# A two-layer attention and expert kernel: the first sequence's tokens sorted into blocks of one expert each, with their rows, weights and first units ahead of the second sequence's chain

## The reference

```
topk_w, topk_idx = top_k(router(x), 2)              # weights made to sum to 1
gate = sum(one_hot(topk_idx, 8) * topk_w, axis=1)
h    = act(einsum('th,ehf->etf', x, W1) + b1)       # relu in layer one, gelu in layer two
y    = einsum('etf,efh->eth', h, W2) + b2
out  = einsum('te,eth->th', gate, y)
```

## Time and profile before

| what | value |
|---|---|
| median of three runs | 1223.13 us (1223.12 to 1223.13) |
| profiled execution, its own time | 1223.02 us |
| its span in the trace | 1221.2 us |
| mean granted PE clock | 0.986 |
| PE busy | 1105.6 us, 91% |
| DVE busy | 864.5 us, 71% |
| ACT busy | 777.3 us, 64% |
| POOL busy | 281.8 us, 23% |
| bytes moved | 57.71 MB, mean 47 GB/s |

### The profile page before, as it was taken

One profiled execution on the slowest core, in us unless ns is written; L12 is line 12 of the kernel. 1 busy time (PEld: TensorE's weight loads), 2 busy tenths in 40 slices (PEclk: granted clock), 3 DMA queues, 4 the chain that ended last, 5 costly groups with the idle time before them and its releaser, 6 DMA issues. The chain is left out here.

```text
span 1221.2 us, 24980 instructions
## 1 busy us (share of the span) xinstructions
PE 1105.6 (91%) x8797; PEld 605.1 (50%) x8872; DVE 864.5 (71%) x2072; ACT 777.3 (64%) x1569; POOL 281.8 (23%) x824
## 2 busy tenths in 40 slices
PE   5899998999999989999988999788888988899996
PEld 3466676655776755666655642222112221137774
DVE  3788767784334467888776889899999989904433
ACT  4366656667444426677666658878888878874443
POOL 8134322333102113433332431111101010100001
PEclk9799999999999999999999999999999989999998
DMA  3444343110000801243312221101111100000000
GB/s 88 118 115 109 96 96 87 49 31 12 1 1 1 184 10 32 59 105 94 85 49 65 55 43 36 24 16 24 36 36 36 23 11 16 7 1 1 10 9 18
DMA packets 40058, 57.71 MB, mean 47 GB/s; under 512 B 9494, under 2 KB 15078, under 8 KB 39678
## 3 DMA queue, kind: packets, MB, share of 16 engines
q1 hardware_dynamic: 39934, 56.11, 18.8%
HBM read 30.81 MB, written 24.64 MB: 45 GB/s over the span
## 5 line engine op out<-in xcount | busy, mean ns | idle before, releaser
L851 ACT ACTIVATE probs<-bank 128x512 f32<-128x512 f32 x1088 | 574.9, 601 | 240.8 <-PE bank L1210 239.8
L950 DVE TENSOR_REDUCE tile_max<-bank 128x1 f32<-128x512 f32 (+3 forms) x1152 | 611.9, 592 | 40.2 <-PE bank L1195 35.6
L1195 PE MATMUL bank<-qk 125*128 125x128 bf16 (+2 forms) x1664 | 389.1, 312 | 66.8 <-DVE tile_max L950 47.0
L1210 PE MATMUL bank<-qk 128*128 128x128 bf16 (+4 forms) x1608 | 362.6, 305 | 5.7 <-ACT probs L851 5.3
L1239 PE MATMUL bank<-probs,v_head 128*32 128x512 f32 (+3 forms) x3328 | 302.9, 453 | 0.1
L1195 PEld LDWEIGHTS bank<-qk 125*128 125x128 bf16 (+1 forms) x1664 | 132.4, 97 | 313.7 <-DVE tile_max L950 243.0
L1117 DVE SCALAR_TENSOR_TENSOR acc<-bank,gate,acc 128x128 f32<-128x128 f32 x256 | 71.9, 343 | 156.7 <-PE bank L1372 156.7
L1239 PEld LDWEIGHTS bank<-probs,v_head 128*32 128x32 f32 x3328 | 139.6, 109 | 52.7 <-issue 29.8
L1210 PEld LDWEIGHTS bank<-qk 128*128 128x128 bf16 (+1 forms) x1664 | 133.1, 97 | 57.2 <-ACT probs L851 21.0
L871 ACT ACTIVATE probs<-bank,sb_b 128x512 f32<-128x512 f32 x128 | 81.0, 684 | 117.9 <-PE bank L1361 117.9
L944 DVE TENSOR_REDUCE tile_max<-bank 128x4 f32<-128x512 f32 x128 | 87.4, 687 | 90.0 <-PE bank L1195 89.9
(11 more groups left out here) (132 smaller groups left out, 664.2 us busy)
## 6 DMA issues: line engine op xcount, KB each, us to landing
qk<-qk_parts SPq DMA_DIRECT2D x160, 144.0 KB
qk_parts<-q_parts SPq DMA_DIRECT2D x48, 192.0 KB, 2.4
qk_parts<-k_parts SPq DMA_DIRECT2D x48, 192.0 KB, 3.2
qk_parts<-q_parts SPq DMA_DIRECT2D x24, 96.0 KB, 2.3
qk_parts<-k_parts SPq DMA_DIRECT2D x24, 96.0 KB, 2.9
sb_w<-in_w SPq DMA_DIRECT2D x8, 256.0 KB, 3.6
sb_w<-in_w SPq DMA_DIRECT2D x2, 1024.0 KB, 5.2
qk<-neg_rows SPq DMA_DIRECT2D x96, 6.0 KB
```

Source lines behind the costliest of these rows:

```text
L851: nc.scalar.activation(probs[:, hd.probs_place(c), :], S2[i % len(S2)][:], ACT.Exp, scale=hd.a.scale).then_inc(sem("probs"), 1)
L950: ins = nc.vector.tensor_reduce(tile_max[:, hd.slot, t, which:which + 1], s1[:, at:at + P * count], AX.X, ALU.max)
L1195: ins = mm(s1[:, at:at + P * count], qk[hd.query_rows, hd.place, 0, P * t:P * (t + 1)], qk[hd.query_rows, hd.place, 1, P * k0:P * (k0 + co ...
L1210: ins = mm(s2[:, at:at + P * count], qk[hd.key_rows, hd.place, 1, P * j:P * (j + 1)], qk[hd.key_rows, hd.place, 0, P * q0:P * (q0 + count) ...
```

## The change

Of the first sequence only the two chosen experts of a token are computed now. The 2 x 1024 pairs of token and expert are sorted by expert into blocks of 128 rows, each block of one expert; in the worst case that makes `BLOCKS` = 23 blocks, so 23 are always computed, four to a unit: 6 units (`BLOCK_UNITS`). The second sequence keeps its 16 units (`dense_unit`), so a layer has 22 in place of 32.

- **Finding the places.** `ranks` (9 small bf16 matmuls with a triangle and ones) counts the tokens of each expert ahead of each token; DVE turns that into starts, the row of each pair (`slots`) and the expert of each block (`blocks`), among the heads.
- **Rows.** POOL issues 16 indirect transfers a layer (`scatter`, 128 rows of 512 bytes each) that write tokens to `x_blocks` in DRAM, cleared beforehand by 23 transfers from `zeros`. In layer two the tokens are first transposed back (`mtok`). SP then loads the rows unit by unit, once all have been scattered, and PE transposes them (`gx`), DVE taking them out of `SHARED`.
- **Weights.** SP first copies W1 and W2 of each expert side by side in DRAM (`put_together`, 16 transfers a layer). A block's weights are then one transfer of 256 KB whose address is a register read from `expert_i`. They land in tensors that are free at that time. In layer one 12 blocks' weights go out under heads 28 to 31, two behind, four behind the rows and five behind the last head; in layer two 18 go out under heads 89 to 94.
- **Results.** DVE copies a block unit's result to `y_out`; SP stores it to `y_blocks`; POOL issues 16 gathers a layer (`gather`), all at one place; DVE adds the two rows of each token, times their weights, to `acc` (`combine`).
- **Order.** Four new places stand in front of a layer's first up (`IN_FRONT`). The turn of the last heads' sums, the rows of blocks 0 to 7 and the transposes `aT` of sequence 1 come there; the rest of its chain goes on through the block units. The gate sums of sequence 0 move from the heads to the units.
- **Transition.** The stores of the first four heads go first, then three heads are loaded, then the other 18 stores.

```diff
-put_routing(0, 0, put_attention_out(0, 0, at_head(17, 1), (0, 1, 2, 4, 5, 7, 8, 10, 11, 12)),
-            (0, 1, 3, 4, 5, 7, 8, 9, 10))
-put_routing(0, 1, put_attention_out(0, 1, at_unit(0, 2, 0)))
+place = put_attention_out(0, 0, at_head(17, 1), (0, 1, 2, 4, 5, 7, 8, 10, 11, 12))
+put_routing(0, 0, place, (0, 1, 3, 4, 5))
+put_places_of_tokens(0, place, (6, 7, 8), 1.78)
...
+first = at_unit(0, -1, 0)
+put(first, ("biases", 0))
+for m, i in enumerate((0, 1, 5, 7, 9, 11)):
+    put(later(first, i), ("gx", 0, m))
+put_attention_out(0, 1, first, (2, 3, 4, 6, 8, 9, 10, 12, 13, 14))
+put_routing(0, 1, first, (14, 15, 15, 16, 16))
+put_gate_sums(0, 1, first, (17, 18, 26, 27))
+put_gate_sums(0, 0, first, (19, 20, 21, 22))
+for c, i in enumerate((24, 29)):
+    put(later(first, 17), ("gather", 0, c))
+    put(later(first, i), ("combine", 0, c))
+    put_next_qkv(c, later(first, i + 1))
...
+            def blocks(f):
+                sp.wait_ge(sem("scattered"), 16 * TOP * TB * (f + 1))
+                for m in range(BLOCK_UNITS):
+                    n = len(blocks_of(m))
+                    sp.dma_start(xg[m][:, 0:P * n].rearrange("p (j d) -> p j d", d=D),
+                                 x_blocks[f].rearrange("(j p) d -> p j d", p=P)[:, TPC * m:TPC * m + n, :]
+                                 ).then_inc(sem(f"x_in{m}"), 16)
+                for j in range(PRELOADS[f][0], PRELOADED, 4):
+                    preload(f, range(j, min(j + 4, PRELOADED)))
+                sp.wait_ge(sem("pv"), BATCHES[RUNS[f].stop])
+                load_block_weights(f, range(PRELOADED, BLOCKS))
...
-            for four in range(len(FOURS)):
+            blocks(0)
+            for p in range(PARTS):
+                store_part(1, 0, 0, p)
+            for g in RUNS[1][0:AHEAD + 1]:
+                load_head(g)
+            for four in range(1, len(FOURS)):
                 for p in range(PARTS):
                     store_part(1, 0, four, p)
-            for g in RUNS[1][0:AHEAD + 1]:
-                load_head(g)
...
+            def scatter(f, i):
+                t = i % TB
+                pool.wait_ge(sem("slots"), f + 1)
+                pool.wait_ge(sem("cleared"), 16 * BLOCKS * (f + 1))
...
+                nc.gpsimd.indirect_dma_start(x_blocks[f], bass.IndirectOffsetOnAxis(ap=places[:, i:i + 1], axis=0),
+                                             tokens_of[:, t, :], None).then_inc(sem("scattered"), 16)
...
                 loaded(pe, f"ffn{f}")
                 pe.wait_ge(sem("max_taken"), CHUNKS[RUNS[f].stop])
+                turn_sums(last)
+                for i in range(IN_FRONT):
+                    between(at_unit(f, -1, i))
                 up(0)
-                turn_sums(last)
```

370 lines of the change are left out of this document (318 added, 52 removed).

## The result

| what | before | changed |
|---|---|---|
| median | 1223.13 us (1223.12 to 1223.44, 4 runs) | 1252.53 us (1251.82 to 1256.27, 4 runs) |
| ratio, 95% interval | | 1.0246 (1.0225 to 1.0266) |
| profiled execution, its span | 1223.02, 1221.2 us | 1252.89, 1250.9 us |

The changed kernel is slower by 29.4 us, where 17.5 less had been forecast. The chip of the result itself isn't on record. Two things have to be told apart, a cost that is there every time and one that came and went.

What follows compares the result with a forecast made beforehand. TensorE was taken to bound causal heads and expert units, VectorE the late heads. Terms, including -8.9 and -15.9 us for the layers, summed to -17.5: 1223.1 to 1205.6 us; range 1191 to 1222, likeliest case 1198 to 1213.

Steps and rivals of the forecast that it cites:

- The gathers: POOL's sixteen indirect loads a layer in the block units: 1.2 us each, hidden, costed at nothing with thin cover.
- Rival 4: POOL's indirect transfers cost more than assumed, deciding from about 1.75 us each; at 2 us, +30 to 1236; chance 0.12.
- VectorE's locks: Part of Rival 4: VectorE's two-port operations stop POOL writing descriptors, bringing the same loss at any transfer cost.
- Heads of run 0: Start and layer-one heads, -1.7 us: gate sums leave, -3.0; small matmuls 0.6, waits 0.4; four scatters fit POOL's 5 us.
- The front of layer one: Between last head and up(0): first rows about 10 us, up(0) at 14.8, TensorE idle +12.6.
- Layer one's units: Front, units and transition, -4.9 us: 10.25 units saved at 3.50, -35.9, against front idle, added TensorE work and waits.
- waits for the shared bank: In block units VectorE empties unit m before taking later rows: 1.3 us idle, four times, +5.1 a layer.
- ScalarE's pieces: Eight pieces a block unit at 0.3 us, 2.4 hidden under 3.50; at 487 ns, 5 us in all.
- Head 32's maxima rows: Transition: SP reaches them 29 us later behind part stores, hidden with 1 to 2 us to spare; +1 us.
- Run 1: Layer-two heads, +3.5 us: VectorE, the bound there, gets 16 operations for ranks, slots and blocks, 4.6 us.
- Layer two: Front and units, -14.4 us: 10.25 units saved, -35.9, against added work, waits, front idle +7.4 and clock +1.5.
- The clock: TensorE drops to a low clock after idle fronts: +3 us in the first layer, +1.5 in the second.

Runs made afterwards that it cites:

- the other chip: Fifth-group rerun of the unmodified changed kernel beside the kernel before: 1214.00 us against 1223.81; the traced execution took 1217.25.
- the sixth group: On one chip: changed kernel rerun, 1249.64 us; changed kernel with loads spread two a unit, later part stores and later norms, 1229.67.
- the fifth group: On one chip: changed kernel rerun, 1214.00 us; its loads on SyncE, 1216.54; kernel before plus sixteen indirect loads, 1224.19, or stores, 1223.46.
- the first group: Changed kernel without indirect transfers, 1207.79 us; with plain POOL transfers, 1210.50; kernel before plus sixteen indirect stores in a row, 1233.84, or POOL subtractions, 1224.42.
- The arithmetic in the heads: Kernel before plus two linked POOL subtractions of 512 columns at each of heads 8 to 23, no transfer: 1228.92 us, ratio 1.0045.
- the fourth group: Changed kernel with scatters replaced by plain SyncE stores after heads 29 and 91, indirect loads kept, no routing into blocks: 1208.19 us, ratio 0.9891.
- the stores made early: Changed kernel with SyncE storing the first sequence's rows in plain transfers after heads 29 and 91 instead of POOL's scatters: 1208.19 us.
- the spread version: Changed kernel with its indirect loads spread two a unit over units 7 to 14, adds and projections later: 1228.29 us, ratio 1.0035.
- second, third and fifth: Separate chips. Second: probe stores in the kernel before, spread loads, 1228.29 us. Third: spread with later stores, 1224.45, plus later norms, 1219.38. Fifth: changed kernel, 1214.00.
- the only spread run with a control: Changed kernel with loads spread two a unit, later part stores and later norms: 1229.67 us beside the unmodified changed kernel at 1249.64.

## Why the prediction was wrong

**The step that failed first was leaving out that another engine's signal could be late.** Every wait in the sum ended with the work item before it. In the result, 36 us of the 47 between the forecast and it are what it took more than the other chip (the two right columns of the table: 1.7, 13.0, 5.0 and 16.3). The 29 in the stages with units stand where waits end with no work item at all; the 6.7 in the heads stand in the stretches with scatters (2.2 and 4.4 in the table of the sixth group). The gathers, "costed at nothing, and the cover is thin", are the term it hangs on. Its durations were right: an issue took 0.96 and 0.30 to the next, 1.26 against the assumed 1.2, sixteen took 20 us, and on the fifth group's chip they did cost nothing. On the chips of the result and of the sixth group the stages with the same sixteen took 12 to 16 us a layer more than there, with the low clock that followed TensorE's waits.

**Rival 4 had the right side and the wrong mechanism.** It was to decide from 1.75 us an issue; with 1.26 it should not have, and didn't. It also said that VectorE's locks would bring the same loss at any price. By the Trainium skill ("SBUF — State Buffer", sections "SBUF: two separate sides" and "Who interferes with whom") the loser of such a lock is POOL or VectorE, and ScalarE never waits for either. The rows show something else: POOL's issues kept their 0.94 to 0.98 us in the traces with late signals as in those without, ScalarE waited as well as VectorE (12.23 and 10.27 us in the first group), and on another chip the same program lost nothing. The loss isn't that one.

**Heads of run 0: -1.7 forecast, +8.9 where no signal was late.** This is a mis-sized term. The forecast let four scatters a head fit into the 5 us that POOL waits for the maxima, (4c - 5) x 4, at c = 1.26 near 0. But POOL's idle time lies ahead of the maxima; work put between the mask and the maxima's parts delays those, and TensorE waits for them. The arithmetic in the heads showed it without a transfer. With the scatters off POOL this stage stood at +3.2 in the fourth group, where its last head ended at 310.78, by the first row below, and at +5.2 in the first. Of the scatters' share 3.2 us can be pinned, the 16.3 against 13.1 in the table of the sixth group. The rest, 5.7, was there without any scatter on POOL or came and went by steps of 1.6 us from one execution to the next, with scatters and without. It comes while the added traffic runs (128 GB/s for 106 in the stretch of the earlier trace rows); which transfer costs it there wasn't tried.

```profile
308.40 2.38 PE L1555 MATMUL bank<-probs,v_head 128*32 128x512 f32 x36
...
314.01 1.11 PE L1658 MATMUL bank<-ident,q_parts 128*128 128x128 f32 x4 [1.58 <-DMA q_parts<-x_blocks]
```

**The front of layer one was right.** Up(0) stood 15.15 us behind the last head (333.28 - 318.13), forecast 14.8; the first rows 8.5 behind it, forecast 10. That the sixteenth scatter holds them is shown by the second row above: with the stores made early the wait for the rows is 1.58 us in place of 6.78, and up(0) stands 11.5 behind the last head, 3.6 sooner than in the fifth group's trace.

**Layer one's units: -4.9 forecast, -7.5 without late signals.** The block units' waits for the shared bank were 0.96 to 1.04 in place of 1.3, and the saving of 3.50 a unit held. ScalarE's pieces took 393 ns, not 300 and not 487: hidden, as said. Head 32's maxima rows cost 0.6 there, forecast 1; the spread version showed how thin that cover was.

**Run 1: +3.5 forecast, +4.6.** The term for VectorE's 16 operations was near enough, and the scatters among these heads cost little where no signal was late: without them the stage took 2.9 more than before in the fourth group and 4.3 in the first. In the result it was +9.6; 4.4 of the 5.0 on top are in the stretch with late signals.

**Layer two: -14.4 forecast, -12.3 without late signals.** Its front was 11.0 in place of 9.6 (up(0) at 1106.48, the last head's end at 1095.45).

**The clock.** In the fifth group's trace the mean granted clock was 0.83 over the 13.5 us behind up(0) in either layer, and 1.00 there before. By that the low clock cost about 2.3 us a layer, an estimate (0.17 of 13.5), where 3 and 1.5 had been forecast. The broken-up second front kept the clock no better than the first.

**The range.** Without late signals the changed kernel took 1214.0, inside 1191 to 1222, by 8 us off the number; there the parts are off in both directions, the heads of run 0 by 10.6 us too low and layer one by 2.6 too high. The range held only what the trace of before could show: an operation that it doesn't contain at all, sixteen in a row beside three engines that hand each other a bank every microsecond, was bounded in its own duration and not in what it does to the others. 0.10 for slower was too little for that.

**What stays open.** That the indirect form is needed is shown on one chip, the first group's: plain stores and loads in rows on POOL, no late signal; sixteen indirect stores, 10 us. No indirect load ran on that chip. What in the chip holds TensorE's signals is open, and why it did so on the chips of the result, of the first and of the sixth group and not on those of the second, third and fifth; the fourth's can't be told. No chip served twice, so a state that a chip was in at the time isn't told from the chip itself. So is whether the count in a row is really what matters: the only spread run with a control moved its adds, projections, stores and norms too.

## What to carry to other kernels

An operation that the trace of before doesn't have needs two prices, what it takes and what it does to engines that don't touch it; the second is measured by adding it alone at a place where nothing depends on it. Put a control, the changed kernel itself, into every group of runs: three experiments here were read as proof of a mechanism that their chip, by its other traces, didn't show. And an engine's idle time is free only where nothing waits for its next step: POOL was idle 5 us a head, and 2 us of work put in at the wrong side of that idle time still cost TensorE time.

## What the runs showed of the hardware

- Indirect transfers of 128 rows of 512 bytes held POOL for 0.94 to 1.01 us (the first of a row up to 1.23) and followed each other every 1.25 to 1.27 in a row; 64 rows took 0.89, plain transfers of the same size 0.55. By the Trainium skill ("DMA: Bandwidth & Descriptors", section on the anatomy of a DMA on the GpSimd path) a transfer takes 2.0 us and its bytes over 436e3, 2.15 for 64 KB; the plain loads landed in 2.2, so row and page agree.
- In three of the seven sets of runs, in rows of them, the signals of TensorE reached VectorE and ScalarE late, by 1.6 us behind four and by up to 12 behind sixteen, while ScalarE's reached TensorE in 0.1 us and POOL's issues kept their length. In three others the same program, or one with the same stores, showed none of it.
- The kernel before took 1223.12 to 1223.44 beside the result, and 1221.6 to 1228.6 on the chips of the experiments, so that a difference of 2 us needs its own group's runs.
